# Six value chunks of a two-layer block as 2x2 block products of seven products, with split weights kept in memory

## What is computed

```python
kk = (h * cm_mk + hh * (1 - cm_mk)) @ Wkey.T        # 2048 x 2048
kv = jax.nn.silu(kk) @ Wval.T                       # 2048 x 512
sr = jax.nn.sigmoid((h * cm_mr + hh * (1 - cm_mr)) @ Wcr.T)
x = x + sr * kv
```

## Time and profile before

| what | value |
|---|---|
| median of 3 runs | 1044.06 us |
| the profiled execution's own time | 1045.26 us |
| span of its trace | 1043.5 us |
| TensorE busy | 1034.6 us, 99% of the span, 4616 matmuls |
| VectorE, GpSimd, ScalarE busy | 714.4, 623.5, 520.7 us |
| DMA moved | 165.60 MB, mean 159 GB/s |

### The profile page before, as it was taken

How to read it: one execution, slowest core, us unless ns; L and a number is a source line. 1 busy time by engine, 2 the same in 40 slices (tenths; PEclk the granted TensorE clock), 3 DMA queues, 4 the chain that set the end, 5 groups by cost and what they waited for, 6 DMA issues and landing times.

```text
span 1043.5 us, 13498 instructions
## 1 busy us (share of the span) xinstructions
PE 1034.6 (99%) x4616; PEld 854.8 (82%) x4616; DVE 714.4 (68%) x1227; ACT 520.7 (50%) x874; POOL 623.5 (60%) x512
## 2 busy tenths in 40 slices
PE   8999999999999999999999999999999999999999
PEld 6777888888888888888888888888888888888887
DVE  7899866786545465466559677688689566666655
ACT  7866888867434354332345434343435344444442
POOL 7796673726756654543537755678683356565652
PEclk9999999999999999999999999999999999999999
DMA  9100315377644343655643764963946445444532
GB/s 349 59 21 0 60 58 127 100 212 269 256 154 160 117 176 119 204 166 147 142 121 113 259 223 162 236 248 128 283 172 204 152 164 176 154 152 161 162 101 81
DMA packets 81124, 165.60 MB, mean 159 GB/s; under 512 B 39073, under 2 KB 39457, under 8 KB 76193
## 3 DMA queue, kind: packets, MB, share of 16 engines
q1 hardware_dynamic: 65600, 116.43, 33.9%
q0 software_dynamic: 15168, 48.24, 15.4%
q10 hardware_dynamic: 288, 0.09, 0.0%
HBM read 101.80 MB, written 58.74 MB: 154 GB/s over the span
## 4 chain that ended last, share of the span: by engine, by line
PE 90%; POOL 4%; DVE 3%; ACT 2%; issue 1%; DMA 0%; SPq 0%; ACTq 0%; DVEq 0%
PE bank L663 15%; PE bank L664 15%; PE bank L665 15%; PE bank L652 13%; PE bank L653 13%; PE bank L654 13%; POOL operand L2039 3%; PE bank L823 2%; PE bank L825 2%; PE bank L824 2%; POOL weights L2027 1%; PE bank L727 1%; ACT made L1003 0%; DVE held L1548 0%; DMA resid<-x 0%
## 5 line engine op out<-in xcount | busy, mean ns | idle before, releaser
L663 PE MATMUL bank<-combo,left 128*128 128x512 f32 x672 | 261.8, 390 | 0.0
L664 PE MATMUL bank<-combo,left 128*128 128x512 f32 x672 | 261.4, 389 | 0.0
L665 PE MATMUL bank<-combo,left 128*128 128x512 f32 x672 | 261.4, 389 | 0.0
L2112 POOL TENSOR_TENSOR inner<-made,inner 128x512 fp32r<-128x512 f32 x96 | 126.9, 1342 | 118.1 <-ACT inner L1147 117.9
L1662 DVE TENSOR_TENSOR resid<-bank,resid 128x512 f32<-128x512 f32 x176 | 119.9, 687 | 112.6 <-PE bank L654 111.6
L2072 POOL TENSOR_TENSOR left<-quart,left 128x512 fp32r<-128x512 f32 x96 | 115.5, 1225 | 82.1 <-ACT left L1114 40.6
L652 PE MATMUL bank<-right,inner 128*128 128x512 f32 x384 | 149.4, 389 | 0.0
L653 PE MATMUL bank<-right,inner 128*128 128x512 f32 x384 | 149.4, 389 | 0.0
L654 PE MATMUL bank<-right,inner 128*128 128x512 f32 x384 | 149.4, 389 | 0.0
L663 PEld LDWEIGHTS bank<-combo,left 128*128 128x128 f32 x672 | 126.2, 188 | 26.9 <-ACT bank L1264 0.4
L665 PEld LDWEIGHTS bank<-combo,left 128*128 128x128 f32 x672 | 126.2, 188 | 26.4
(11 more groups left out here) (199 smaller groups left out, 1966.9 us busy)
## 6 DMA issues: line engine op xcount, KB each, us to landing
kept_left<-left SPq DMA_DIRECT2D x24, 1792.0 KB, 8.0
left<-kept_left POOLq DMA_DIRECT2D x24, 1024.0 KB, 7.2
left<-kept_left POOLq DMA_DIRECT2D x24, 768.0 KB, 5.0
quart<-wide SPq DMA_DIRECT2D x24, 512.0 KB, 4.1
tall_staged<-tall SPq DMA_DIRECT2D x48, 256.0 KB, 5.4
raw<-kept SPq DMA_DIRECT2D x32, 256.0 KB, 6.1
landed<-wts SPq DMA_DIRECT2D x20, 256.0 KB, 5.9
resid<-x POOLq DMA_DIRECT2D x4, 1024.0 KB, 9.3
```

The costliest lines, as they stand in the source:

```text
L663: pe.matmul(acc[:], hi, combo[:, c, k, 0, :], start=fresh and k == 0, stop=False, skip_group_check=True)
L664: pe.matmul(acc[:], hi, combo[:, c, k, 1, :], start=False, stop=False, skip_group_check=True)
L665: mm = pe.matmul(acc[:], lo, combo[:, c, k, 0, :], start=False, stop=k == 1, skip_group_check=True)
L2112: pool.tensor_tensor(inner[:, h % 4, i, 1, :], made_at(n), inner[:, h % 4, i, 0, :].bitcast(F32), ALU.subtract).then_inc(inner_lo, 1)
```

## The change

Chunks 0 to 5 of the second pair's value product (made in units 8 to 13) are no longer made by `out_tile` but by feature as 12 **groups**: two for a chunk, and a group gives 128 output features of each half of the 512 for both token blocks of the pair, as a 2x2 block product of seven products of three matmuls. Units 9 to 14 run a new order on ScalarE, VectorE and GpSimd (`value_unit`), and TensorE has two group steps in each of a unit's seven gaps (`value_slot`), from the third gap of unit 9 to the second gap of unit 15; before, each of units 9 to 15 had eight tiles, and now unit 15 alone still has them (chunk 6), with chunk 7 in units 16 to 18, as before. So there are 48 fewer tiles of 6 matmuls (288) and 12 x 7 x 3 = 252 new matmuls. For a chunk ScalarE makes seven high parts (`value_hi_of`), GpSimd seven low parts, VectorE the sums T1 and T3 and GpSimd T2 and T4 out of the four silu tiles.

The split weights and their four sums for these groups are made in units 0 to 6, beside the first pair's value product of the same weights (`quarters_summed_of` on VectorE, `summed_hi_of` on ScalarE, `summed_lo_of` on GpSimd), stored by ten DMAs a unit on the SP queue (`keep_right`, 1.8 MB) and loaded back by GpSimd's queue in two halves of 896 KB a chunk (`load_value`). The second pair's x1 is turned to features by VectorE (`x_turned_of`, units 0 and 1) and moved into memory by 32 DMAs of 128-byte runs (`move_x`, units 1 to 4) in place of the 32 DMAs that moved its squares from SBUF to SBUF in units 22, 23, 27 and 28; the channel receptance of the second pair is made by feature. `load_raw` moves to unit 5, `right_sums` of stage 1 from unit 4 to unit 6, and `load_tall` waits for the four sums of the chunk before. The statistics of the second pair are now by runs of 32 features, joined by 16 small DMAs (`move_stats`). `PIECES_AT` takes the place of `piece_at`. Three weight matrices are awaited whole instead of by quarters.

```diff
+VALUE_CHUNKS = 6
+VALUE_UNIT = KEY_UNITS + 1
+VALUE_GROUPS = 2 * VALUE_CHUNKS
+PLAIN_UNIT = KEY_UNITS + VALUE_CHUNKS
...
+VALUE_MADE = (B11, T3, T2, B21, T1, T4, B22)
+TILE_CHUNKS = LAST_CHUNK - VALUE_CHUNKS
...
+def value_steps(u, slot):
+    first = 2 * SEVEN * (u - VALUE_UNIT) + 2 * (slot - 2)
+    return [divmod(n, SEVEN) for n in (first, first + 1) if 0 <= n < SEVEN * VALUE_GROUPS]
...
+PIECES_AT = ((18, 18, 19, 20, 21, 22, 23), (21, 22, 24, 25, 26, 27, 27),
+             (35, 37, 39, 41, 43, 45, 47), (43, 45, 47, 49, 51, 53, 55, 59, 61))
+STATS_PIECE = (SUBS, SUBS, SUBS + 2, SUBS + 2)
...
+            def move_x(b, sources):
+                sp.wait_ge(x_turned, SUBS * (b - 1))
+                for a in sources:
+                    for c in range(SQUARES):
+                        source = raw[3 - b][a * SQUARE:(a + 1) * SQUARE].rearrange("q k (s t) -> q (k s) t", s=SUBS)
+                        goal = kept_x1[b][c * SQUARE:(c + 1) * SQUARE].rearrange("q k (s t) -> q (k s) t", s=SUBS)
+                        sp.dma_start(goal[:, :, a * SQUARE:(a + 1) * SQUARE],
+                                     source[:, :, c * SQUARE:(c + 1) * SQUARE]).then_inc(xt_kept, 16)
...
+            def keep_right(u):
+                sp.wait_ge(summed_lo, u + 1)
+                if u:
+                    sp.wait_ge(right_lo, 2 * u)
+                else:
+                    sp.wait_ge(first_right_lo, 2)
+                for m in range(2):
+                    goal, columns = kept_right[u][:, m], slice(m * P, (m + 1) * P)
+                    lower = slice(HALF + m * P, HALF + (m + 1) * P)
+                    sp.dma_start(goal[:, :, A22, :], right[:, u % 2, 1, :, lower].bitcast(F32)).then_inc(right_kept, 16)
+                    for part in range(2):
+                        sp.dma_start(goal[:, part, A11:A22, :],
+                                     right[:, u % 2, :, part, columns].bitcast(F32)).then_inc(right_kept, 16)
+                        sp.dma_start(goal[:, part, S1:SEVEN, :],
+                                     summed[:, u % 2, part, :, columns].bitcast(F32)).then_inc(right_kept, 16)
...
+                if q < VALUE_GROUPS:
+                    kk, m = divmod(q, 2)
+                    pe.wait_ge(value_lo, value_made(kk, c))
+                    pe.wait_ge(value_loaded[m], 16 * (kk + 1))
+                    hi, lo = (value_right[m][:, part, a, :] for part in range(2))
+                    plain, rest = (value_at(c, part) for part in range(2))
...
+            def value_slot(u, slot):
+                for q, step in value_steps(u, slot):
+                    (side_1, side_7, side_6, side_2, side_5, side_4, side_3)[step](q)
...
                 product(X, u, A11, B11, True).then_inc(p1, 1)
+                value_slot(u, 0)
...
                 product(V, u, S3, T3, True).then_inc(p7, 1)
+                value_slot(u, 1)
...
+            def value_hi_of(kk, c):
+                if kk:
+                    act.wait_ge(value_used[c], 2 * kk)
+                else:
+                    act.wait_ge(out_psum, FIRST_TILES - (2 * SUBS if c == B11 else 0))
+                if c in (T1, T3):
+                    act.wait_ge(value_sums, 2 * kk + (T1, T3).index(c) + 1)
+                elif c in (T2, T4):
+                    act.wait_ge(value_later, 2 * kk + (T2, T4).index(c) + 1)
+                else:
+                    act.wait_ge(silu_done, silu_by(KEY_UNITS + kk, (B11, B21, B22).index(c)))
+                act.activation(value_at(c, 0), value_plain(c), ACT.Copy).then_inc(value_hi, 1)
...
+            def value_unit(u):
+                kk, q, last = u - VALUE_UNIT, 2 * (u - VALUE_UNIT), u == PLAIN_UNIT
+                value_hi_of(kk, T3)
+                act.wait_ge(p1, u + 1)
+                act.wait_ge(silu_done, silu_by(u - 1, 3))
+                act.activation(Y[:], X[:], ACT.Copy).then_inc(x_copied, 1)
+                value_hi_of(kk, T2)
+                value_hi_of(kk, B21)
+                value_hi_of(kk, T1)
+                act.wait_ge(p7, u + 1)
+                act.wait_ge(v_summed, u)
+                act.activation(seventh[:], V[:], ACT.Copy).then_inc(seventh_copied, 1)
+                group_copied(q)
+                group_seventh(q)
+                value_hi_of(kk, T4)
+                value_hi_of(kk, B22)
+                act.wait_ge(p2, u + 1)
+                key_silu(u, 0, X)
+                act.wait_ge(p4, u + 1)
+                key_silu(u, 1, Z)
+                act.wait_ge(v_summed, u + 1)
+                key_silu(u, 2, V)
+                group_copied(q + 1)
+                if last:
+                    key_inner_hi(u, 0)
+                    unit_right_hi(u)
+                    group_seventh(q + 1)
+                    act.wait_ge(p3, u + 1)
+                    key_silu(u, 3, Y)
+                else:
+                    value_hi_of(kk + 1, B11)
+                    act.wait_ge(p3, u + 1)
+                    key_silu(u, 3, Y)
+                    group_seventh(q + 1)
...
+                    if u == KEY_UNITS:
+                        value_hi_of(0, B11)
...
+            def quarters_summed_of(u):
+                a11, a21 = tall_staged[0][:, 0:HALF], tall_staged[0][:, HALF:H]
+                a12, a22 = tall_staged[1][:, 0:HALF], tall_staged[1][:, HALF:H]
+                s1, s2, s3, s4 = (summed_plain[:, u % 2, 1, n, :] for n in range(QUARTERS))
+                for i in range(2):
+                    dve.wait_ge(tall_loaded[i], 16 * (u + 1))
+                dve.wait_ge(x_turned, SUBS * min(u + 1, PAIRS))
+                if u >= 2:
+                    dve.wait_ge(right_kept, RIGHT_KEPT * (u - 1))
+                dve.tensor_tensor(s1, a21, a22, ALU.add).then_inc(quarters_summed, 1)
+                dve.tensor_tensor(s3, a11, a21, ALU.subtract).then_inc(quarters_summed, 1)
+                dve.wait_ge(quarters_summed, 4 * u + 1)
+                dve.tensor_tensor(s2, s1, a11, ALU.subtract).then_inc(quarters_summed, 1)
+                dve.wait_ge(quarters_summed, 4 * u + 3)
+                dve.tensor_tensor(s4, a12, s2, ALU.subtract).then_inc(quarters_summed, 1)
...
+            def value_unit(u):
+                kk, q = u - VALUE_UNIT, 2 * (u - VALUE_UNIT)
+                value_sum(kk, T1)
+                if kk:
+                    seed_side(q - 1)
+                value_sum(kk, T3)
+                if kk:
+                    add_x(q - 1)
+                    add_y5(q - 1)
+                    add_v(q - 1)
+                    add_z(q - 1)
+                    add_y3(q - 1)
+                seed(u)
+                last_norm(u, 0)
+                seed_side(q)
+                add_x(q)
+                sum_v(u)
+                add_y5(q)
+                add_v(q)
+                add_z(q)
+                if u in SUMS_UNIT:
+                    dve.wait_ge(value_lo, value_made(kk, T1))
+                    right_sums(SUMS_UNIT.index(u))
+                add_y3(q)
+                last_norm(u, 1)
...
+            def load_value(q):
+                kk, m = divmod(q, 2)
+                if q < 2:
+                    pool.wait_ge(out_psum, FIRST_TILES - (2 * SUBS if q == 0 else 0))
+                else:
+                    pool.wait_ge(o3, q - 1)
+                pool.wait_ge(right_kept, RIGHT_KEPT * (kk + 1))
+                pool.dma_start(value_right[m][:], kept_right[kk][:, m]).then_inc(value_loaded[m], 16)
...
+            def value_unit(u):
+                kk = u - VALUE_UNIT
+                pool.wait_ge(value_sums, 2 * kk + 1)
+                pool.tensor_tensor(extra[:, 1, :], made[:, 2, :], extra[:, 0, :], ALU.subtract).then_inc(value_later, 1)
+                value_lo_of(kk, T3)
+                value_lo_of(kk, T2)
+                for j in range(PAIRS):
+                    if 2 * u == stats_at(j) + 1:
+                        norm(2 * BLOCKS + j)
+                value_lo_of(kk, B21)
+                pool.wait_ge(value_later, 2 * kk + 1)
+                pool.tensor_tensor(made[:, 1, :], made[:, 1, :], extra[:, 1, :], ALU.subtract).then_inc(value_later, 1)
+                load_value(2 * kk + 1)
+                value_lo_of(kk, T1)
+                value_lo_of(kk, T4)
+                value_lo_of(kk, B22)
+                for j in range(PAIRS):
+                    if 2 * u == stats_at(j):
+                        norm(2 * BLOCKS + j)
+                if u < PLAIN_UNIT:
+                    load_value(2 * kk + 2)
+                    value_lo_of(kk + 1, B11)
+                    load_left(u + 2)
+                else:
+                    key_inner_lo(u, 0)
+                    unit_right_lo(u)
...
+                        if piece > STATS_PIECE[j] and j >= PAIRS:
+                            norm3_rows(j, KT // 2 + piece - STATS_PIECE[j] - 1)
```

More of the change, by code:

```diff
@@ L516, in load_tall @@
             def load_tall(u):
-                for t in (2 * u, 2 * u + 1) if is_key(u) else (KEYS + u,):
+                if 0 < u <= VALUE_CHUNKS:
```

(36 more changed lines are left out.)

464 lines of the change are left out of this document (315 added, 149 removed).

## The result

The changed kernel takes 1078.94 us (median of 4 runs, 1077.42 to 1082.2) against 1044.09: a ratio of 1.033 (95% interval 1.0317 to 1.0343), 34.9 us slower. The forecast was 1043.7 in 1038.0 to 1049.5, so the time lies far outside the range, on the side to which 0.26 was given. The profiled execution took 1077.72 us with a span of 1075.9, 32.4 more than that of the kernel before.

A forecast was written before the change was run, and what follows sets the result against it. TensorE, busy 99%, was taken to bound the kernel: 36 fewer matmuls save 8.16 us, waits and small edits take back 7.7, so 0.4 us less, 1043.7 us, range 1038.0 to 1049.5.

The forecast's parts named there:

- A: Unit 9, p6: TensorE waits for ScalarE's copy of X, now behind T3's split copy; 0.8 us.
- B: Unit 9, side_5: seed_side comes late behind two make_x2 and a bn_stats on VectorE; 0.9 us (0.1 to 2.1).
- C: Unit 11, side_5: 4.1 us of norm work stands ahead of seed_side on VectorE; 0.8 us (0.1 to 1.6).
- D: Unit 14, side_5 of unit 13's second group: seed_side late behind norm3 and transposes; 1.3 us with refill (0.9 to 2.1).
- E: End of unit 14: right_sums ahead of add_y3 delays freeing OY; 0.8 us (0.5 to 3, if right_sums waits for squares).
- G: Units 29 to 32: moved norm3_rows piece ahead of right_sums makes seed late for p5 of unit 31; 2.8 us (1.5 to 3.8).
- F: Kept weights for the value units: loads land in 6 us, in time; 0 us, or 0.2 to 1.2 in six units at 7.2.
- the edits costed at 0.3 together: Units 0 to 8's added work, queue issues and moved squares fall into idle time; 0.3 us together, bounds 0 to 3.
- The rival of the shared port: Value units: most VectorE operations on two SBUF tiles wait for a GpSimd operation; 5.4 us more, 1049.1 us; chance 0.17.

The follow-up runs named there:

- e5: Changed kernel with norm work of units 9 to 13 laid into gaps, add_y3 ahead of right_sums, second block's squares a unit earlier: 1065.53 us.
- e1: Changed kernel with GpSimd's subtractions for T1, T4 and B22 in unit 11 cut to 8 of 512 columns: 1074.01 us.
- e11: e9 with GpSimd's T2 sum in units 10 to 14 waiting for VectorE's T3: 1042.79 us, ratio 0.9977 to the kernel before.
- e3: Changed kernel with add_y3 ahead of right_sums on VectorE in unit 14: 1079.53 us, ratio 1.0315 to the kernel before.
- e8: Changed kernel with the edits of e5 and e6 together, plus three edits of order in units 1 and 9: 1057.07 us.
- e2: Changed kernel with move_stats issued behind keep_left and load_fin of its unit on SP: 1073.68 us, ratio 1.0272 to the kernel before.
- e6: e2 with the second pair's statistics a unit earlier and its last row at half unit 59: 1068.13 us, ratio 1.0229 to the kernel before.
- e9: e8 with a second layout: unit 9's load_value(1) first on GpSimd, T2 on VectorE, seed_side ahead of T1, last load_rows behind the quarter load: 1043.57 us.
- e10: Kernel before the change, with ScalarE repeating the copy of X in five units so that TensorE pauses: 1067.97 us (one run).
- e4: Changed kernel with the second pair's last norm3_rows on VectorE at half unit 59 instead of 61: 1073.94 us, ratio 1.0287 to the kernel before.

## Why the prediction was wrong

**What held.** The matmuls are 4580, TensorE's steps are as costed, and all of A, B, C, D, E and G showed up at the place and with the waiting instruction that the text named. D was right in size: 1.5 for 1.3. F cost nothing, as forecast: the load of unit 9 landed after 5.0 where 6 was taken. Its premise, no load just ahead of it, is what e5 broke.

**What failed.** The waits come to 33.7 us over their forecast: A, B and C 13.3, the edits costed at 0.3 together 12.2, E 5.0, G 3.0, D 0.2. Of these 33.7, 11.9 are the lower clock. The steps of the text that made them:

**A, B and C: the price of one meeting.** The text gave a VectorE operation that meets GpSimd 1.0 us more, from the 1.71 of the earlier trace rows, as one GpSimd instruction is 1.28 long, and let one of four meet. What the runs showed: make_x2 waited 3.7 and 2.7 us for a run of three subtractions, the norm3 pair, which reads one tile, met them as well (2.95 for 0.99), and T3 took 1.82. The rival of the shared port had the mechanism, at 0.17, and was itself priced by single meetings, 5.4 us; A, B and C came to 15.8 with the clock. e1 shows it by itself for unit 11, e11 for T3. By the Trainium skill (SBUF — State Buffer, Who interferes with whom) a two-input VectorE instruction and a GpSimd instruction that reads SBUF exclude each other for one whole instruction, the first to issue going first. The trace agrees on the exclusion (T3, 0.69 or 1.82) and differs on its length: in units 9 and 11 VectorE waited for three. It does not show who issued first in unit 9: the record of the multiplication starts at 428.15, ahead of GpSimd's 428.23, but the operation ahead of it ends at 428.23 as well.

**E: the squares.** Their sixteen issues were costed by the 11.46 of the earlier trace rows and the 2.3 of the earlier trace rows; they took 15.01 and 2.9. `right_sums` was thus 17.9 us behind the last transpose and not 13.8. In those 15 us the DMA engines moved 236 GB/s, in the 11.46 of the kernel before 90; that this is why the issues took longer is not shown. The upper bound of 3 was the right mechanism; e3 shows that the order on VectorE would not have saved it, e5 that earlier squares do.

**Edits at 0.3 together.** Two of these sentences failed. Of the "four sums a unit of the kind that took 0.42" three took 1.5 beside GpSimd's splits in unit 1, and ScalarE's copy of them stood ahead of the copy of X of unit 1: 2.3 us, gone in e8. "Moving 32 squares out of units 22 to 28 and 16 small DMAs in ... is 0": the small DMAs are sixteen for each block, 32 in all, issued in one go. The first sixteen pushed keep_left against the quarter load, 4.4 (e2). And load_rows, which waits for GpSimd's last row of the block before, stood in front of another quarter load, 5.8: with the statistics a unit earlier that wait stayed (e6), with load_rows behind the load it went (e9). I had counted the issues and not looked at what would stand behind them in SP's order.

**G: mechanism right, size off.** 4.1 for 2.4 at p5, because two splits of combinations behind the piece met GpSimd too (3.46 at 815.49, for 1.28 at 785.13 in the kernel before), and 1.7 of slow steps.

**No term for the clock.** 11.9 us of the 41.4 are slow steps behind six of the nine waits; the text had some 0.4 of refill in D and 0.1 in G. Those six waits of 2.7 to 5.0 us cost 1.6 to 3.0 on top. e10 shows the lower clock behind pauses in a kernel without the change.

What stays open: why VectorE waited for a whole run of subtractions in units 9 and 11, while in unit 1, in e4 and just ahead in unit 9 itself (1.16 and 1.66) the two engines took turns, one instruction each.

## What to carry to other kernels

Where TensorE is at 99%, count an edit's gain first and then ask of each instruction that it moves what stands behind it in the same queue, SP's loads above all: in the changed kernel 36 of the 43 us between its time and the full gain came back by moving lines (e11). Lay VectorE's operations on two SBUF tiles into the stretches in which GpSimd has no run of its own, and price a meeting by the whole run as the upper bound. The six waits of the changed kernel that lowered TensorE's clock cost half as much again (11.9 us behind 23.6), its three shorter ones 0.1 each; so short waits were cheaper than a long one of the same sum.

## What the runs showed of the hardware

The clock behind a pause: over all runs, each of the 24 waits of 3.5 us and more (but the one ahead of the first matmul) was followed by steps of 427 ns, 1.5 to 3.0 us lost; of those between 1.9 and 3.5 us some were and some were not (1.95 us in unit 29 of e1 was, 3.0 in e10 and 3.4 in e6 were not); none under 1.9 us was. So the length of the wait alone does not decide it in between.

A load's time to land depends on what was sent out just ahead of it. On its own queue: 10.0 us for a quarter load behind 1.8 MB and three loads of 256 KB, 3.5 behind sixteen small ones and one of 256 KB (e2). On another queue: 9.4 us for kept weights on GpSimd's queue behind six loads of 256 KB on SP's (e5), 5.0 where those came after it.
